# Recurrent block with a routed feed-forward part: routing prefix one chunk sooner, positions in parts of 8 to 16 tiles, and the transition between the two halves reordered

## The reference, cut to what matters

```python
x = L0_attn_x                        # (32, 256, 128) float32, 8192 rows of 128
xn = layernorm(x)                    # over the last axis
# the recurrent half
hidden, gate = split(xn @ W_hg)      # 2 x 256 columns
a = sigmoid(-gate); v = (relu(hidden) + 0.5) * sigmoid(gate)
h[t] = a[t] * h[t - 1] + v[t]        # along each of the 32 sequences
s = h @ W_out
# the feed-forward half: one shared expert, and the best 2 of 16 for each row
shared = (silu(xn @ Sg) * (xn @ Su)) @ Sd
probs = softmax(xn @ Wr)             # 16 experts
routed = sum over the two best e of probs[e] * ((silu(xn @ Wg[e]) * (xn @ Wu[e])) @ Wd[e])
out = x + s * silu(routed + shared)
```

## Time and profile before

| what | us |
|---|---|
| device time, median of 3 runs | 327.69 (325.77 to 329.65) |
| device time of the profiled execution | 327.45 |
| span of the profiled execution | 325.7 |
| PE busy | 291.7 (90%) |
| DVE busy | 252.0 (77%) |
| ACT busy | 241.4 (74%) |
| POOL busy | 201.2 (62%) |

### The profile page before, as it was taken

The page is one execution under the profiler, slowest core; times in us unless marked ns, Lnnn a source line. Parts: engine busy times, 40 slices in busy tenths (PEclk is TensorE's granted clock), DMA queues, the critical chain, the costliest instruction groups (busy, mean ns, idle before and its releaser), DMA issues.

```text
span 325.7 us, 5997 instructions
## 1 busy us (share of the span) xinstructions
PE 291.7 (90%) x1523; PEld 198.5 (61%) x1523; DVE 252.0 (77%) x634; ACT 241.4 (74%) x517; POOL 201.2 (62%) x242
## 2 busy tenths in 40 slices
PE   0699999999989999996968999999999999999920
PEld 0357767766656666663645676777777777777620
DVE  7399999999999799999451778787878787878830
ACT  1789999999975777985664777777787878787520
POOL 3997446530137776878667777665656566656670
PEclk9999999999998999998999999999999999999985
DMA  8999999690006885333795435755656454541000
GB/s 233 303 372 393 440 445 399 228 432 3 0 28 204 279 256 215 124 127 147 247 405 195 168 107 194 208 176 149 180 149 181 150 181 129 168 127 51 19 0 0
DMA packets 28256, 63.62 MB, mean 195 GB/s; under 512 B 3717, under 2 KB 22672, under 8 KB 27456
## 3 DMA queue, kind: packets, MB, share of 16 engines
q1 hardware_dynamic: 21184, 45.58, 41.3%
q0 software_dynamic: 6752, 17.06, 14.2%
q10 hardware_dynamic: 288, 0.60, 0.6%
HBM read 29.32 MB, written 35.14 MB: 198 GB/s over the span
## 4 chain that ended last, share of the span: by engine, by line
PE 78%; ACT 5%; issue 5%; POOL 4%; DVE 3%; DMA 1%; POOLq 0%; ACTq 0%; DVEq 0%
PE p_u L998 21%; PE p_u L926 20%; PE p_s L1023 10%; PE p_s L937 8%; PE p_sh L1010 5%; PE p_lg L907 4%; PE p_sh L946 4%; PE p_xt L974 3%; POOL out L354 2%; PE p_xt L894 2%; DMA arena<-in_x 1%; POOL arena L310 1%; ACT arena L457 1%; ACT rec L427 1%; ACT rec L420 1%
## 5 line engine op out<-in xcount | busy, mean ns | idle before, releaser
L354 POOL DMA_INDIRECT out<-arena x83 | 82.1, 989 | 46.4 <-DVE arena L825 30.0
L926 PE MATMUL p_u<-xT,w_front 128*128 128x512 f32 x192 | 93.9, 622 | 3.2 <-DVE prod L569 2.5
L348 POOL DMA_INDIRECT slots<-arena,pos x64 | 71.4, 1116 | 28.7 <-issue 16.1
L998 PE MATMUL p_u<-arena 128*128 x166 | 78.3, 593 | 0.0
L926 PEld LDWEIGHTS p_u<-xT,w_front 128*128 128x128 f32 x192 | 34.9, 198 | 35.4 <-issue 33.9
L1023 PEld LDWEIGHTS p_s<-arena,rec 128*128 128x128 f32 x332 | 43.4, 191 | 21.2 <-issue 21.2
L799 DVE TENSOR_TENSOR rec<-p_u,rec 128x512 f32<-128x512 f32 (+1 forms) x42 | 28.8, 685 | 29.3 <-ACT rec L473 29.3
L480 ACT ACTIVATE rec<-p_sh 128x512 f32<-128x512 f32 (+1 forms) x42 | 24.9, 592 | 30.8 <-PE p_sh L1010 30.8
L1023 PE MATMUL p_s<-arena,rec 128*128 x332 | 44.1, 276 | 1.3 <-ACT rec L480 1.3
L998 PEld LDWEIGHTS p_u<-arena 128*128 128x128 f32 x166 | 28.3, 190 | 19.6 <-issue 19.6
L561 DVE TENSOR_TENSOR_SCAN rec<-rec 128x512 f32<-128x512 f32 x32 | 39.3, 1229 | 1.1
(11 more groups left out here) (130 smaller groups left out, 440.5 us busy)
## 6 DMA issues: line engine op xcount, KB each, us to landing
slots<-arena SPq DMA_DIRECT2D x4, 4116.0 KB, 27.0
arena<-slots SPq DMA_DIRECT2D x41, 392.0 KB, 3.3
arena<-in_W_lines SPq DMA_DIRECT2D x2, 2304.0 KB, 11.3
arena<-in_x SPq DMA_DIRECT2D x16, 256.0 KB, 5.3
arena<-in_W_lines SPq DMA_DIRECT2D x4, 768.0 KB, 4.5
out<-arena POOLq DMA_INDIRECT x83, 2.7
slots<-arena,pos POOLq DMA_INDIRECT x64
w_front<-in_W_front ACTq DMA_DIRECT2D x1, 392.0 KB, 3.6
```

Source lines behind the costliest of these rows:

```text
L348: pool.indirect_dma_start(slots, index, xrow[:, t], None).then_inc(s_disp[t % WINDOW], 16)
L354: pool.indirect_dma_start(out, index, xg[:, n % RX, h, X], None, bounds_check=T - 1, oob_is_err=False)\
L926: nc.tensor.matmul(p_u[:, n % 4], w_front[:, UPS[q]:UPS[q] + P], xT[:, c % XB], start=True, stop=True)\
L998: last = nc.tensor.matmul(p_u[:, n % 2 * 2 + h], xsT[:, n % 2, h * P:(h + 1) * P], w_lines[:, bass.DynSlice(line_at[2 * n + h], 4 * P)], s ...
```

## The change

1. `HALVES` becomes `PARTS`: the positions of group 0 come in parts of 8, 16 and 16 tiles, those of group 1 in two parts of 12. Each part stands behind `shared_gated` of a chunk (chunks 6, 7, 8, 13 and 14).
2. The first `prefix` stands in chunk 6, after the transposes. The others of group 0 stand behind the last product of chunks 7 and 8.
3. Logits of chunks 13, 14 and 15 are no longer made in chunks 6, 7 and 8, but together in chunk 9, with one copy.
4. Each group has its own tables `oh`, `cum`, `carry` (41 and 25 columns for each line), set up by POOL at the start; the second group's scan has 500 columns and not 820.
5. Row statistics run one chunk further ahead (`STATS`, 6 buffers and not 4).
6. The transition: `tile_keys` of both groups (which fill `toff`) come after the last chunk on DVE; PE's register loads come ahead of the first transpose; `rec_down` and `shared_down` of the last chunk come between the first and the second transpose; ACT normalises pair 0 ahead of the last `shared_silu`.

```diff
-    HALVES = [[(0, 20), (20, 40)], [(0, 24)]]
+    PARTS = [[(0, 8), (8, 24), (24, 40)], [(0, 12), (12, 24)]]
...
-        PREFIX_AFTER = [13, 14]
-
-        STATS = {i: [2 * i + 5, 2 * i + 6] for i in range(-1, 5)} | {5: [15]}
+        EARLY_LOGITS = READ[5][-1] + 1
+        LATE_LOGITS = list(range(EARLY_LOGITS, NCH))
+
+        STATS = {-1: [3, 4, 5]} | {i: [2 * i + 6, 2 * i + 7] for i in range(5)}
...
-            nc.gpsimd.memset(carry[:, :, :], 1.0).then_inc(s_const0, 1)
-            nc.gpsimd.memset(oh[:, :, :], 0.0).then_inc(s_const, 1)
-            pool.wait_ge(s_const0, 3)
-            nc.gpsimd.memset(carry[:, :, 0:1], 0.0).then_inc(s_const, 1)
+            for g in range(2):
+                nc.gpsimd.memset(carry[g][:, :, :], 1.0).then_inc(s_const0, 1)
+                nc.gpsimd.memset(oh[g][:, :, :], 0.0).then_inc(s_const, 1)
+            pool.wait_ge(s_const0, 4)
+            for g in range(2):
+                nc.gpsimd.memset(carry[g][:, :, 0:1], 0.0).then_inc(s_const, 1)
...
+                if i == NCH - 1:
+                    copy_down(i - 1)
+                    normalise_slots(0)
                 shared_silu(i)
-                if i >= 1:
+                if 1 <= i < NCH - 1:
                     copy_down(i - 1)
...
-            for n in range(2):
+            copy_slot_xT(0)
+            for n in range(1, 3):
                 normalise_slots(n)
-                copy_slot_xT(n)
             copy_down(NCH - 1)
+            copy_slot_xT(1)
...
-                if i == 7:
-                    key_bases(0)
-                    positions(0, 0)
-                if i == 8:
-                    positions(0, 1)
                 if i == 9:
-                    tile_keys(0)
...
                 if i == 13:
                     key_bases(1)
-                    positions(1, 0)
-                if i == 14:
-                    tile_keys(1)
...
-                if read(i):
+                if i <= 5:
                     copy_logits(read(i))
                 if i == 6:
                     probabilities(0)
                 shared_gated(i)
+                if i == 6:
+                    key_bases(0)
+                if 6 <= i <= 8:
+                    positions(0, i - 6)
+                if i == 9:
+                    copy_logits(LATE_LOGITS)
                 if i == 12:
                     probabilities(1)
+                if 13 <= i <= 14:
+                    positions(1, i - 13)
+            for g in range(2):
+                tile_keys(g)
...
-                if first > PREFIX_AFTER[0]:
-                    pe.wait_ge(s_pos, first - PREFIX_AFTER[0])
+                if first == EARLY_LOGITS:
+                    pe.wait_ge(s_pos, len(PARTS[0]))
...
-                pe.wait_ge(s_lgc, NCH if g else PREFIX_AFTER[k] + 1)
+                pe.wait_ge(s_lgc, NCH if g else EARLY_LOGITS)
                 if g or k:
-                    pe.wait_ge(s_pos, len(HALVES[0]) if g else k)
+                    pe.wait_ge(s_pos, len(PARTS[0]) * g + k)
...
-                if i in (7, 8):
-                    prefix(0, i - 7)
...
+                if i == 6:
+                    prefix(0, 0)
+                if i == 14:
+                    prefix(1, 1)
                 up(i, 4)
                 up(i, 5)
-                if read(i):
+                if i <= 5:
                     logits(read(i))
-            first_slots()
+                if i in (7, 8):
+                    prefix(0, i - 6)
+                if i == 9:
+                    logits(LATE_LOGITS)
+            load_keys(0)
+            slot_transpose(0)
             rec_down(NCH - 1)
             shared_down(NCH - 1)
+            slot_transpose(1)
+            gate_up(0)
+            load_keys(1)
```

86 lines of the change are left out of this document (36 added, 50 removed).

## The result

| | before | after |
|---|---|---|
| median of 18 runs each, us | 328.75 (325.77 to 331.57) | 323.76 (322.12 to 325.97) |
| profiled execution, us | 327.45 | 322.83 |
| its span, us | 325.7 | 321.1 |
| POOL busy, us | 201.2 | 200.7 |
| PE's share of the chain that ended last | 78% | 61% |

The ratio to the kernel before is **0.990, 95% interval 0.988 to 0.993**: 3.2 us less (2.4 to 4.0). I had forecast 5.2 us. In this ratio and in all that follow, runs more than 1.5% above the fastest of their own kernel are left out, which drops 5 of the 18 runs of before, from the upper of its two usual levels (near 327.6 and near 330.5), and none of the changed kernel; the medians given are those of all runs, here 5.0 us apart.

What follows compares the result with a forecast made beforehand. It took PE as the bound, with POOL's dispatch chain hidden close beside it. PE would gain 8.0 us, but POOL's 2.0 + 2.1 + 1.1 allowed only 5.2: 327.45 - 5.2 = 322.3 us, range 318.8 to 325.5.

Steps and rivals of the forecast that it cites:

- the price of the two stops: PE's stops in chunks 8 and 15 go, worth 3.2 and 4.2 us, of which 1.7 each is lost clock.
- the spare of POOL's chain: At the load of pair 11, POOL's chain has 2.1 us to spare, plus 1.1 from ACT and PE.
- the last sum: Second half comes sooner by 2.0 (POOL's chain) + 2.1 + 1.1 (spare) = 5.2 us before PE waits for pair 10 or 11.
- PE's 8.0: PE alone reaches the first slots 8.0 us sooner: +1.0 - 3.2 - 4.2 - 1.6.
- Start, +1.0: POOL's added table set-up ahead of the bias of chunk 2 makes all of the first half 1.0 us later.
- First dispatch 1.4 us sooner, at 92.7: POOL's first dispatch: shorter first positions and no copied logits ahead, less the 1.0 us start; bounds 0 and 2.6.
- the late case: Rival: POOL comes no sooner, only 3.2 us are left, 324.2 us; sign: first dispatch at or after 94; chance 0.22.
- Dispatch pace, -0.6: On POOL, three dispatches or so go at the faster pace once DVE's scans are over: 0.6 us sooner.
- my slower case: Rival: DVE runs late and four waits for positions all stop PE, +6.8 us, 334.2 us; chance 0.06.
- Transition 8.6 us, 3.0 of it standing: From end of chunk 15 to gate_up(1): 8.6 us, not 10.2; -1.6, or 0 if the standing lowers the clock.
- New stop at pair 10 to 12, released over a store and a load: Sign in the second half: PE stops 1 to 3 us, released through a slot load by an output store.
- PE sets the time: Rival: POOL has more to spare or gains more, so PE's gain of 6.3 to 8.0 us shows; chance 0.22.

Runs made afterwards that it cites:

- b2: Kernel before with only the transition of the change (both key computations behind chunk 15, new ACT and PE orders): 328.97 us beside 329.72, ratio 1.000.
- b1: Kernel before with two dead fills of 500 columns added on POOL ahead of rstd_of(2): ratio 1.002 to before.
- a0: Changed kernel, unchanged, timed and traced again: 324.64 us against 329.78 of before, ratio 0.992.
- a3: Changed kernel with two dead fills (1.23 us together) on POOL between the dispatches of the two groups: 325.0 us beside 324.64 of a0.
- c0: Kernel before, unchanged, traced again and timed against itself: ratio 0.995.
- a1: Changed kernel with the second group's tables set up on POOL behind rstd_of(2) instead of ahead of it: 323.5 us, ratio 0.988 to before.
- v1: Changed kernel with 12 buffers for the rows of the slots instead of 10: 322.85 us, ratio 0.984 to before.
- b3: Kernel before with two dead fills on POOL between the dispatches of the two groups: 330.09 us beside 329.72, ratio 1.004.
- e1: Changed kernel with a stop put back on PE in chunk 7, ahead of prefix(0, 1): 325.31 us beside 323.65 of e0, ratio 1.005.
- e0: Changed kernel, unchanged, on the same chip as e1: 323.65 us, ratio 0.988 to before.

## Why the prediction was right and wrong

**The step that failed** is the price of the two stops, "So the two stops cost 1.52 + 1.7 = 3.2 and 2.46 + 1.7 = 4.2 us", and with it the spare of POOL's chain, the 2.1 + 1.1 of the last sum, read from the same execution. At equal clock the stretches to chunk 7 and from 7 to 10 shrink by 0.8 + 0.6 = 1.4 us (28.2 to 27.64; the stop was 1.52) and that from 10 to 15 by 2.7 (42.4 to 39.74; the stop was 2.46). So the two are worth about 4.1 us and not 7.4. The 1.7 + 1.7 us of clock that I added (1.66 and 1.47 by the table) were falls of the traced execution: b2 has the same stops and neither fall, b1 has one, and a0 and a3 lose 1.7 us in chunks 9 and 10 without a stop. Crediting the change with one execution's falls made PE's 8.0 too large (4.2 by the table, an estimate: 322.5 below against 22.13 + 68.70 + 27.64 + 39.74 + 11.13 + 149.0 = 318.3), and the 2.1 + 1.1 us of spare hold PE's lateness by those falls. By spans the spare was 3.6 us in that trace, which agrees with my 3.2, but 1.2 in c0, 1.0 in b1 and 0.4 in b2. The falls are only a part of this. In b2 PE ended 1.4 us sooner than in the first trace, but POOL's first store came 1.8 us later. And c0, the same kernel with two falls as well, lost its spare to POOL alone: 96.96 us from first to last dispatch, where the first trace has 94.80. In these traces POOL waited 6.5 us (before), 8.3 (c0) and 9.7 (b2) for landings of earlier dispatches; why these vary stays open.

In the pair of first traces the last sum fails by its other term. POOL's first store came 1.0 us sooner and not 2.0, since its start was late, and 1.0 + 3.6 = 4.6 is the measured difference of the spans. That a forecast of 5.2 lies so near this 4.6 is partly luck, as both traces of the pair could have been others.

What the sum gives without falls, an estimate from the table: before 21.07 + 69.49 + 28.21 + 42.41 + 12.84 + 148.5 = 322.5; the changed kernel by POOL's chain with the first store of a0, 187.22 + 131.9 = 319.1. That is 3.4 us, beside the 3.2 us of the ratio. The agreement leans on a0, whose POOL chain is the quickest of all; with the first stores of the two other traces, 189.16 and 190.25, it would be 1.5 and 0.4 us. The 3.2 us are a mean over such executions, and the sum does not prove them.

Point by point:

- **Start, +1.0**: right where the clock rises early (b1, a1), nothing where it rises late.
- **First dispatch 1.4 us sooner, at 92.7**: 92.61 and 92.67 in a0 and a3, with the early rise as in the trace of before (94.11); 93.73 in the traced execution of the change, whose rise was late. By the letter of my test ("a first dispatch at or after 94") it was not the late case, by 0.3 us.
- **Dispatch pace, -0.6**: from first dispatch to last 94.80 us before, 94.05 after. Right in these two, but the same distance is 93.35 in a0, 96.7 in v1 and 97.0 in c0, so the term is smaller than its own scatter.
- **Stops gone**: right, clock 1.00 and no stop over 0.36 us from 89 to 162 us. The four waits for positions of my slower case never stopped PE. The Trainium skill (VectorE: DVE Perf Modes, rules for kernel authors) would charge the split for its 12 added instructions; no stretch of this table shows that charge: PE's longest wait for DVE in these chunks is the 0.36 us, and DVE's busy time as a whole went from 252.0 to 250.9 us.
- **Transition 8.6 us, 3.0 of it standing**: 8.4 and 3.27 at full clock, right (the old order took 10.1 and not 10.2: my 177.3 is the end of the transpose, `gate_up(1)` starts at 177.16). "Or 0 if the 3 us of standing lower the clock once more" was too small: a0, a3 and b2 show the fall, and a0 lost 2.8 us by it, so with it the new order takes 13.85 to 14.15 us, 1.0 to 1.3 more than the 12.84 of before. The old order has falls too (14.24 in b3). Behind `gate_up(1)` the new order takes 0.5 us more (149.0 against 148.5, with b2 as well); 0.4 of it lies between `gate_up(1)` and `gate_up(2)`, where PE now waits 0.27 us for DVE (`rec`, line 807). Alone it is worth nothing in the mean (b2, 1.000).
- **New stop at pair 10 to 12, released over a store and a load**: right, pair 10, 1.28 us. I had reckoned with pair 11 and the store alone. Pair 10 is also the first that waits for the last dispatch, 1.4 us ahead of the first store in POOL's order; v1 shows that taking the store away leaves the stop in an execution whose last dispatch is late (190.76).
- **The rivals**: "PE sets the time" (0.22) is not another outcome but the other kind of execution of the same kernel (a0, a3). I gave one chance to each where both occur.

## What to carry to other kernels

Before the clock that a stop lost is added to the price of the stop, look at more than one trace: the same kernel, traced again, may lose it elsewhere or not at all, and every distance to spare that is read from that trace holds the loss as well. When a second chain (here POOL's dispatches) ends within a few us of the first, a change has two prices, one for each kind of execution; shorten both chains or expect the smaller gain. And time the kernel before against itself once: the 0.995 that came out here is as large as several of the differences between variants. A wait on a load is worth reading to its last condition: two that come within 1.4 us of each other hide one another.

## What the runs showed of the hardware

- PE starts at half pace, and the moment at which it comes to full pace differs between executions of one kernel. The four `up` products ahead of mark 1 that start at 16.7 and 16.6 us in before and a0 took 1.88 us; in the first trace of the changed kernel they took 2.98 us (timeline of PE):

```profile
17.94 2.98 PE L926 MATMUL p_u<-xT,w_front 128*128 128x512 f32 x4
```

  Four such products took 3.78 us at half pace (start at 11.91), so full pace came at about 15.5 us in before and 21.2 in c0, the same kernel, whose four at 17.91 took 3.54: an estimate from these lengths. Mark 1 shifts by 1.1 (a0 to after) to 2.7 us (before to c0). The Trainium skill (TensorE: Matmul & The Clock Gate, Part 1) says that the monitor behind the clock runs freely and is not reset when a kernel starts, and gives 0.5 us either way for the variation. The traces agree that the moment varies from run to run, but by more than 5 us, and the measurement decides.
- The clock fell in chunks 9 and 10 of a0 and a3 (0.83 over 110 to 120 us) with PE busy for 10.00 of 10 us there and 29.00 of 29 around it. I had not expected a fall without a stop, and no run here explains it. Both came to full pace at nearly the same moment (second row of `up` products at 16.61 and 16.60 us).
- It stayed up behind stops of 1.52, 2.10 and 2.47 us (b2, e1) and in some executions behind one of 3.27 to 3.47 us (after, v1, e0), and fell behind one of 3.47 in a0 and 3.22 in b2. The length of a stop alone did not decide it.
